# Cross attention block 4: rows of queries and keys interleaved, scores later behind the maxima, another order of loads, half of the last projection inside the block

## The chip, the cores and the metric

One core of one Trainium2 chip runs the whole program. The metric is the device time of one execution in microseconds, of which the span from the first to the last instruction is the larger part. TensorE (PE) multiplies matrices, VectorE (DVE), ScalarE (ACT) and GpSimd (POOL) work elementwise, and DMAs are issued from the queues of SyncE (SP) and of POOL.

## What is computed

Six residual blocks over x of shape (8, 100, 256): self attention with a learned position term, a cross attention, a mixture of experts, a gated scan, a second cross attention, and a projection with ternary weights. The change touches the last two:

```python
def _L1_xattn_ref(query, key, value, mask, ...):   # 16 heads of 16, 8 batches, 100 queries, 361 keys
    q = _split_heads(query @ Wq.T + bq)
    k = _split_heads(key @ Wk.T + bk)
    v = _split_heads(value @ Wv.T + bv)
    scores = jnp.einsum('bhtd,bhsd->bhts', q, k) * scale
    scores = jnp.where(mask[:, None, None, :], scores, -jnp.inf)
    attn = jax.nn.softmax(scores, axis=-1)
    out = jnp.einsum('bhts,bhsd->bhtd', attn, v)
    return out.transpose(0, 2, 1, 3).reshape(...) @ Wo.T + bo

x = x + _L1_xattn_ref(_layernorm(x), ctx_1024, ctx_1024, mask_BxS2_bk0, ...)
x = x + _L1_ffn_ref(_layernorm(x), L1_ffn_weight)   # one 256 x 256 projection
```

## The kernel before

The program counts its blocks from 0: the second cross attention is block 4, the last projection block 5. X holds the residual stream, 100 tokens on partitions for each of 8 batches; a "half" is four batches.

Block 4 works in bf16 with each fp32 number of the queries and keys split into three bf16 parts. Six products of parts (PARTS) are kept, so the contraction of a score has 6 x 16 rows, one row with the mask (ROW_MASK, row 96) and, in the second pass, three rows with the negated row maximum (ROW_MAX, rows 97 to 99). The operands lie in QS (all queries, in region RC) and KS (four slots of one batch each, in regions RBG and RA). The parts go from on-chip memory to DRAM (q_parts, k_parts) and come back, one DMA for each of the six groups of 16 rows: load_queries (L412) and load_keys (L426, and L429 for the mask row). SP issues the queries and keys 0 to 3, POOL keys 4 to 7, each when the scores of the batch two before are over and behind its own four small operations on the maxima.

For each batch and pair of heads, "maxima" (L1259) multiplies queries and keys once and DVE reduces the result to a negated row maximum NM (L1604). POOL splits NM in three (L723 to L726), PE transposes it ("parts", L1270), ACT copies it to NT (L906) and SP stores it in rows 97 to 99 of QS (load_maxima, L419). Then "scores" (L1286) multiplies again, transposed and with the maximum taken off, twelve units in a batch, ACT takes the exponential (L899), "weighted" (L1299) multiplies by the values, and sums_tr (L1311), normalise (L1613, L1614), out_tr (L1319), ot_evac (L920), out_mm (project, L951) and add (L1387) finish the batch. DVE then takes the statistics for the next layer norm (L1350, L1354), POOL the power -0.5 (L598).

The order on each engine comes from a table of ticks, PLAN, walked by run_block4: batch b's entry stands at its tick plus 16 b, and every engine picks its own entries in that order. A tick is no time, only a place in the order. The part of the table before:

```python
        PLAN = ([("maxima", 2 * i, i) for i in range(PAIRS)]
                + [("parts", 21, 0)]
                + [("scores", 28 + TICKS * u // UNITS4, u) for u in range(UNITS4)]
                + [("weighted", max(35 + u // 2, 32 + TICKS * u // UNITS4), u) for u in range(UNITS4)]
                + [("os_evac", 46, 0), ("sums_tr", 49, 0), ("normalise", 49, 0), ("out_tr", 56, 0),
                   ("out_mm", 58, 0), ("add", 59, 0)])
```

After the table block 5 runs: for each half eight transposes (L940), one evacuation to XT (L744), four projections (L951) and four adds, and out goes batch by batch (L570).

## Time and profile before

| | |
|---|---|
| time before, median of 3 (lowest, highest) | 506.22 us (499.56, 510.32) |
| profiled execution: time, span | 508.15 us, 506.4 us |
| mean granted TensorE clock | 0.885 |
| busy over the span | PE 429.4 us (85%), DVE 265.5 (52%), ACT 163.3 (32%), POOL 130.1 (26%) |
| chain that ended last | PE 65%, DVE 11%, DMA 10%, POOL 6%, ACT 4% |
| blocks 0 to 3 | up to 330 us |
| block 4, first maxima to last output projection | 352 to 492 us |

The profile page cuts the span into 40 slices of 12.7 us. The row of TensorE's granted clock reads nine or ten tenths for most slices up to 342 us, and then 5 7 9 5 7 9 5 9 8 9. The chain of waits is read from the last instruction back: at each step to what released it. [...]

### The profile page before, as it was taken

Reading aid. Unit: us, or ns where it says so; the run is one execution under the profiler, and the core shown is the slowest. Engines: PE = TensorE matmul, PEld = TensorE weight load, DVE = VectorE, ACT = ScalarE, POOL = GpSimd, SP = SyncE. Lnnn points to the kernel's source line nnn. Section 1 sums busy time; section 2 is a strip of 40 time slices with the busy share of each in tenths; the row PEclk is TensorE's granted clock in tenths of the full one; section 3 lists DMA queues with packets and bytes.
Section 4 is the critical chain, followed back from the end, with each engine's and each line's share of the span. In section 5 each row is a group of like instructions: output and inputs, shape, how many; then the busy total and the mean of one; then the engine's idle time right before and its main releaser. Section 6 shows DMA issues by size and latency. Waiting matters only on the chain.

```text
span 506.4 us, 7332 instructions
## 1 busy us (share of the span) xinstructions
PE 429.4 (85%) x2920; PEld 280.8 (55%) x2920; DVE 265.5 (52%) x481; ACT 163.3 (32%) x334; POOL 130.1 (26%) x174
## 2 busy tenths in 40 slices
PE   2999986959999974997999999961979969979986
PEld 1556743535667754874555557640346646646654
DVE  5056676992146520236675998651953634643423
ACT  0440430004531231322537424021143534523731
POOL 4620075327441066056100000006003213300100
PEclk9999998969999886999999999995575795975989
DMA  8991020001116963320000029976175256320002
GB/s 242 363 246 37 1 63 27 0 0 45 44 45 192 370 262 113 84 71 20 1 2 0 0 37 134 126 128 90 37 111 75 38 71 91 62 31 2 3 1 65
DMA packets 30616, 42.17 MB, mean 83 GB/s; under 512 B 4330, under 2 KB 27286, under 8 KB 30186
## 3 DMA queue, kind: packets, MB, share of 16 engines
q1 hardware_dynamic: 28279, 35.95, 28.6%
q0 software_dynamic: 2304, 5.76, 7.1%
q8 instruction: 23, 0.38, 0.4%
q14 instruction: 10, 0.08, 0.1%
HBM read 33.00 MB, written 8.98 MB: 83 GB/s over the span
## 4 chain that ended last, share of the span: by engine, by line
PE 65%; DVE 11%; DMA 10%; POOL 6%; ACT 4%; issue 3%; SPq 1%; ACTq 0%; DVEq 0%; POOLq 0%
PE banks L1193 13%; PE banks L1259 6%; PE banks L951 5%; PE banks L1299 5%; PE banks L1286 5%; DMA RC<-NT 4%; PE banks L1006 4%; PE banks L980 3%; PE banks L1227 3%; PE banks L940 2%; DVE RA L449 2%; PE banks L1031 2%; PE banks L1112 2%; PE banks L1130 2%; DMA RC<-q_parts 2%
## 5 line engine op out<-in xcount | busy, mean ns | idle before, releaser
L1604 DVE TENSOR_REDUCE NM<-banks 100x2 f32<-100x722 f32 x64 | 57.2, 906 | 63.2 <-PE banks L1259 62.4
L1193 PE MATMUL banks<-XT,RBG 128*128 128x400 f32 x192 | 65.0, 500 | 2.1 <-ACT XT L744 2.1
L1193 PEld LDWEIGHTS banks<-XT,RBG 128*128 128x128 f32 x192 | 36.3, 190 | 29.8 <-issue 1.2
L899 ACT ACTIVATE CT<-banks 128x400 f32<-128x400 f32 (+1 forms) x72 | 35.9, 504 | 41.9 <-PE banks L1286 40.8
L598 POOL TENSOR_TENSOR rstd<-ve,mhalf 100x4 f32<-100x4 f32 x12 | 12.5, 1040 | 140.0 <-DVE ve L1359 140.0
L744 ACT ACTIVATE XT<-banks 128x800 f32<-128x800 f32 x14 | 11.6, 838 | 98.6 <-PE banks L940 98.6
L1259 PE MATMUL banks<-RBG,RC 97*100 97x361 bf16 x64 | 23.1, 464 | 13.6 <-DMA RC<-q_parts 12.2
L940 PE MATMUL banks<-identf,XN 100*128 100x100 f32 x112 | 17.1, 309 | 17.5 <-DVE XN L1364 10.0
L1299 PE MATMUL banks<-CT,RV 128*17 128x100 f32 (+1 forms) x576 | 28.4, 293 | 0.0
L1286 PE MATMUL banks<-RC,RBG 100*128 100x100 bf16 (+1 forms) x192 | 21.7, 254 | 7.6 <-DMA RC<-NT 7.6
L1286 PEld LDWEIGHTS banks<-RC,RBG 100*128 100x128 bf16 (+1 forms) x192 | 18.3, 140 | 15.4 <-DMA RC<-NT 8.7
L940 PEld LDWEIGHTS banks<-identf,XN 100*128 100x128 f32 x112 | 14.4, 175 | 21.5 <-issue 10.9
L723 POOL CAST NP<-NM 100x16 bf16<-100x16 f32 x8 | 1.6, 196 | 96.2 <-DVE NM L1604 96.2
L980 PE MATMUL banks<-CT,W 128*128 128x361 f32 x64 | 24.5, 536 | 1.9 <-ACT SELT L766 1.9
L1079 PE MATMUL banks<-RC,SELT 128*128 128x400 f32 x64 | 23.7, 518 | 2.7 <-DVE RC L1445 2.4
L1405 DVE TENSOR_TENSOR RC<-RV 128x800 f32<-128x800 f32 x16 | 15.3, 999 | 18.3 <-ACT RV L786 15.9
L1387 DVE TENSOR_TENSOR X<-X,banks 100x256 f32<-100x256 f32 x32 | 13.3, 415 | 21.9 <-PE banks L951 16.9
L1350 DVE BATCH_NORM_STATS2 st<-X 100x6 f32<-100x256 f32 x48 | 19.9, 425 | 7.2 <-DMA X<-in_x 5.8
L636 POOL TENSOR_TENSOR RA<-RA 128x722 f32<-128x722 f32 x6 | 9.0, 1506 | 52.3 <-ACT RA L766 52.3
L991 PE MATMUL banks<-W,CT 128*128 128x256 f32 (+1 forms) x96 | 21.8, 387 | 0.5 <-DVE RC L1533 0.5
L1286 PE MATMUL banks<-RC,RA 100*128 100x100 bf16 (+1 forms) x192 | 18.6, 227 | 4.1 <-DMA RC<-NT 4.1
L1259 PE MATMUL banks<-RA,RC 97*100 97x361 bf16 x64 | 21.5, 429 | 0.0
(228 smaller groups left out, 832.8 us busy)
## 6 DMA issues: line engine op xcount, KB each, us to landing
RA<-in_L_ffn_W SPq DMA_DIRECT2D x2, 2048.0 KB, 11.8
k_parts<-RA SPq DMA_DIRECT2D x18, 180.5 KB, 3.4
RBG<-in_L_attn_W_aiv SPq DMA_DIRECT2D x1, 3072.0 KB, 16.1
CT<-in_ctx_t SPq DMA_DIRECT2D x2, 1444.0 KB, 11.4
RC<-q_parts SPq DMA_DIRECT2D x12, 200.0 KB, 6.7
RBG<-k_parts SPq DMA_DIRECT2D x12, 180.5 KB, 8.8
RA<-k_parts SPq DMA_DIRECT2D x12, 180.5 KB, 9.1
RBG<-k_parts POOLq DMA_DIRECT2D x12, 180.5 KB, 6.5
```

The source lines that it names most:

```text
L899: sc.activation(P4[slot][0:n, g * HG * T:(g + 1) * HG * T], PS[4 + w % 2][0:n, 0:HG * T], ACT.Exp).then_inc(st_exp, 1)
L940: ins = nc.tensor.transpose(PS[2 * g + k][:, j * T:j * T + T], XN[:, b, k * P:(k + 1) * P], identf[0:T, 0:T])
L951: ins = mm(bank[0:T, 0:D], lhs(k), rhs(k), start=(k == 0), stop=(k == KT - 1))
L980: ins = mm((lo, hi)[m][:, 0:S], W4[:, 0, k, m * P:(m + 1) * P], CT[:, k, b * S:(b + 1) * S], start=(k == 0), stop=(k == KT - 1))
L991: ins = mm(o, CT[:, k, b * S + s0:b * S + s0 + n], W4[:, 1, k, :], start=(k == 0), stop=(k == KT - 1))
L1006: ins = mm(PS[4 + i % 2][:, 0:GC], W0[:, w, k, m * P:(m + 1) * P], XT[:, k, GC * g:GC * g + GC], start=(k == 0), stop=(k == KT - 1))
L1079: ins = mm(PS[2 * (u % 3) + g][:, 0:GC], SELT[:, u], AL[:, GB * g:GB * g + GB].rearrange("p s t -> p (s t)"), start=True, stop=True)
L1193: ins = mm(PS[2 * aiv_pair(i) + g][:, 0:GC], WA[:, k, c:c + P], XT[:, k, GC * g:GC * g + GC], start=(k == 0), stop=(k == KT - 1))
L1259: ins = mm(PP[w % 2][0:T, c, 0:S], queries(ROW_MAX, h, b), KS[b % KSLOTS][0:ROW_MAX, h, :], start=True, stop=True)
L1286: ins = mm(PS[4 + w % 2][0:n, c * T:c * T + T], KS[b % KSLOTS][0:KROWS, h, s0:s0 + n], queries(KROWS, h, b), start=True, stop=True)
L1299: ins = mm(PS[6][32 * c:32 * c + VW, g * T:g * T + T], V4[0:n, NJ * b + j, h, :], P4[(NJ * b + j) % PSLOTS][0:n, h * T:h * T + T], start=( ...
L1604: v.tensor_reduce(NM[:, b % 2, 2 * i:2 * i + 2], PP[w % 2][0:T, :, 0:S], AX.X, ALU.max, negate=True).then_inc(mx_out, 1)
```

## The change

Five edits. The rows of part product r go to partitions r, r + 6, r + 12, ... instead of 16 r to 16 r + 15, in QS and KS alike, so the contraction is the same sum in another order. In the table, everything from scores on stands eight ticks later. Keys 2 and 3 are issued after the first half's queries, and keys 3 after the first negated maxima. The half 0 part of block 5 is put into the table at ticks 134 to 146, with semaphores of its own, and the statistics of a batch are closed at once. Waits follow: parts waits for an add three batches back.

```diff
-        PLAN = ([("maxima", 2 * i, i) for i in range(PAIRS)]
-                + [("parts", 21, 0)]
-                + [("scores", 28 + TICKS * u // UNITS4, u) for u in range(UNITS4)]
+                + [("scores", 36 + TICKS * u // UNITS4, u) for u in range(UNITS4)]
...
+        ONCE = ([("ffn_tr", 134, 0), ("ffn_xt", 136, 0)] + [("ffn_mm", 138 + 2 * b, b) for b in range(GB)]
+                + [("ffn_add", 140 + 2 * b, b) for b in range(GB)])
...
-                    queue.dma_start(QS[DK * r:DK * r + DK, g].rearrange("d (k h) n -> d k (h n)", h=HK),
+                    queue.dma_start(QS[r:ROW_MASK:len(PARTS), g].rearrange("d (k h) n -> d k (h n)", h=HK),
...
-                queue.dma_start(KS[s][DK * r:DK * r + DK].rearrange("d (k h) s -> d k (h s)", h=HK),
+                queue.dma_start(KS[s][r:ROW_MASK:len(PARTS)].rearrange("d (k h) s -> d k (h s)", h=HK),
...
-            sp.wait_ge(state, RT)
-            for b in (2, 3):
-                key_ones(b)
-                load_keys(sp, b)
-
             sp.wait_ge(y_mm, 3 * B)
...
+            sp.wait_ge(state, RT)
+            key_ones(2)
+            load_keys(sp, 2)
+            for i in range(3):
+                sp.wait_ge(q4_split1, max(i, 1))
+                store_queries(1, i)
+            for i in range(3):
+                load_queries(sp, 1, i)
             for b in range(B):
 
                 sp.wait_ge(np_out, b + 1)
                 for i in range(3):
                     load_maxima(sp, b, i)
                 if b == 0:
-
-                    for i in range(3):
-                        sp.wait_ge(q4_split1, max(i, 1))
-                        store_queries(1, i)
-                    for i in range(3):
-                        load_queries(sp, 1, i)
+                    key_ones(3)
+                    load_keys(sp, 3)
...
-                if b >= 2:
-                    pe.wait_ge(on_ready, b - 1)
+                if b >= 3:
+                    pe.wait_ge(x_new, 4 * B + b - 2)
...
+            def ffn_tr(_):
+
+                pe.wait_ge(mx_out, PAIRS * B)
+                pe.wait_ge(wf_ready, 1)
+                transposes(5 * B, 0)
+
+            def final(b, bank):
+                pe.wait_ge(xt_ready, 5 * KT * G + KT * (b // GB + 1))
+                for k in range(KT):
+                    ins = mm(bank[0:T, 0:D], XT[:, k, b * T:b * T + T], WN[:, k, :], start=(k == 0),
+                             stop=(k == KT - 1))
+                ins.then_inc(y5_mm, 1)
+
+            def ffn_mm(b):
+                if b >= 2:
+                    pe.wait_ge(x5_new, b - 1)
+                final(b, PS[2 + b % 2])
...
+            pe.wait_ge(x5_new, GB)
+            transposes(5 * B, 1)
+            for b in range(GB, B):
+                final(b, PS[b])
...
-                if L + 1 >= NBLOCKS:
+                if L + 2 == NBLOCKS:
+                    stats(L + 1, b)
+                    aggregate(L + 1, b)
+                    if b == GB - 1:
+                        variance(L + 1, 0)
+                    if b == GB:
+                        norm(L + 1, 0)
+                    if b == B - 1:
+                        variance(L + 1, 1)
+                        norm(L + 1, 1)
                     return
```

How the instructions move, in three places. A row names the line, the operation, its output and inputs by region, the output's shape and how many stand in a row; an fp32 matmul counts once here and twice in the trace. Line numbers of the changed kernel are its own.

TensorE from the last query projection to the first scores, before:

```order
L1239 MATMUL banks<-XT,W 128x400 x4
L1259 MATMUL banks<-RBG,RC 100x361 x22
L1270 MATMUL banks<-identb,NP 48x100
L1259 MATMUL banks<-RBG,RC 100x361 x8
L1286 MATMUL banks<-RC,RBG 128x100 x8
```

and of the change:

```order
L1247 MATMUL banks<-XT,W 128x400 x4
L1267 MATMUL banks<-RBG,RC 100x361 x22
L1278 MATMUL banks<-identb,NP 48x100
L1267 MATMUL banks<-RBG,RC 100x361 x10
L1267 MATMUL banks<-RA,RC 100x361 x6
L1294 MATMUL banks<-RC,RBG 128x100 x4
```

Maxima (L1259, now L1267) come in twos, one pair of heads: 15 pairs stood ahead of the first scores (L1286, now L1294), and now 19; 4 pairs lay between the transpose of the first negated maxima (L1270, now L1278) and the first scores, and now 8.

SP's queue from the loads of keys to the second half's queries, before (keys 2 and 3 go to RA, queries to RC):

```order
L529 DMA RA<-ones_d 3x5776
L426 DMA RA<-k_parts 16x2x2888 x6
L429 DMA RA<-mask_d 1x16x361
L546 DMA RC<-ones_d 1x12800
L525 DMA q_parts<-WX 128x2x400 x3
L412 DMA RC<-q_parts 16x2x3200 x6
L419 DMA RC<-NT 1x16x100 x3
```

and of the change:

```order
L549 DMA RC<-ones_d 1x12800
L533 DMA q_parts<-WX 128x2x400 x3
L420 DMA RC<-q_parts 16x2x3200 x6
L537 DMA RA<-ones_d 3x5776
L434 DMA RA<-k_parts 16x2x2888 x6
L437 DMA RA<-mask_d 1x16x361
L533 DMA q_parts<-WX 128x2x400 x3
L420 DMA RC<-q_parts 16x2x3200 x6
L427 DMA RC<-NT 1x16x100 x3
```

The key loads that stood ahead of the first query store stand behind the first query loads, and the second half's stores and loads moved ahead of the first negated maxima (RC<-NT).

TensorE's end, before (L940 transposes, L951 with WN the last projection):

```order
L1319 MATMUL banks<-identf,zrow 128x100 x2
L951 MATMUL banks<-W,PEM 100x256 x2
L940 MATMUL banks<-identf,XN 128x100 x8
L951 MATMUL banks<-WN,XT 100x256 x8
L940 MATMUL banks<-identf,XN 128x100 x8
L951 MATMUL banks<-WN,XT 100x256 x8
```

and of the change:

```order
L1319 MATMUL banks<-PICK,WQK 100x68 x4
L1327 MATMUL banks<-identf,zrow 128x100 x2
L959 MATMUL banks<-W,PEM 100x256 x2
L948 MATMUL banks<-identf,XN 128x100 x8
L1343 MATMUL banks<-WN,XT 100x256 x8
```

One of the two sets of eight transposes and four projections is gone from the end; it stands between the scores of batches 6 and 7.

## Rows read from the trace of the kernel before

**Rows 1.** The page's costliest groups: line, engine, shapes, count | busy, mean ns | idle before

```profile
L1604 DVE TENSOR_REDUCE NM<-banks 100x2 f32<-100x722 f32 x64 | 57.2, 906 | 63.2 <-PE banks L1259 62.4
```

**Rows 2.** The chain that ended last, in order of time: start us, us, what

```profile
336.31 4.15 DMA q_parts<-WX
...
342.71 9.34 DMA RC<-q_parts
...
373.55 6.71 DMA RC<-NT
...
400.43 0.44 PE banks L1259 x2
...
406.83 8.10 DMA RC<-NT
...
430.33 1.96 PE banks L951 x4
...
441.13 7.79 DMA RC<-NT
```

**Rows 3.** Who waited for whom, 330 to 507 us: total us, times, longest us

```profile
PE banks L1259 <- DMA RC<-q_parts: 12.2, 1, 12.2
PE banks L1286 <- DMA RC<-NT: 11.7, 3, 4.1
```

**Rows 4.** Stretches: length, each engine's busy us (instructions), PEclk, DMA share, GB/s

```profile
12.00:25.00 13.00, 12.16 (x31) 6.69 (x31) 0.46 (x2) 5.50 (x8) 8.83 (x13) 1.00 1.06 366
344.00:350.00 6.00, 0.00 (x0) 0.00 (x0) 0.00 (x0) 0.00 (x0) 5.86 (x4) 0.50 0.98 123
352.10:365.80 13.70, 12.14 (x32) 3.97 (x33) 11.98 (x14) 1.53 (x2) 1.51 (x5) 0.50 0.01 3
381.00:398.00 17.00, 17.00 (x157) 11.12 (x150) 6.14 (x8) 6.73 (x15) 4.45 (x11) 0.50 0.50 68
415.00:432.30 17.30, 17.30 (x160) 11.37 (x161) 6.14 (x8) 6.87 (x15) 4.30 (x11) 0.51 0.46 67
432.30:445.00 12.70, 12.63 (x191) 8.74 (x189) 9.16 (x14) 7.69 (x17) 4.31 (x11) 0.99 0.56 82
449.00:466.10 17.10, 17.10 (x160) 11.28 (x161) 6.14 (x8) 6.87 (x15) 0.82 (x4) 0.52 0.01 2
492.36:506.40 14.04, 9.38 (x48) 6.96 (x46) 5.89 (x17) 1.67 (x2) 1.01 (x1) 0.95 0.20 58
```

**Rows 5.** Short stretches at edges of the granted clock, same columns

```profile
340.00:343.50 3.50, 0.02 (x1) 0.00 (x0) 0.00 (x0) 1.68 (x4) 0.00 (x0) 1.00 0.83 173
343.50:344.50 1.00, 0.00 (x0) 0.00 (x0) 0.00 (x0) 0.37 (x1) 0.56 (x1) 0.60 1.15 134
370.00:372.00 2.00, 2.00 (x40) 1.20 (x33) 1.10 (x2) 0.82 (x2) 0.00 (x0) 0.75 1.07 128
490.50:491.00 0.50, 0.50 (x2) 0.36 (x3) 0.00 (x0) 0.00 (x0) 0.00 (x0) 0.50 0.00 0
```

**Rows 6.** POOL in order of time: start us, us, what

```profile
385.04 3.14 POOL L426 DMA_DIRECT2D RBG<-k_parts  x6
388.13 0.53 POOL L429 DMA_DIRECT2D RBG<-mask_d  x1
```

**Rows 7.** DMA issues (384 to 400 us, then 320 to 507 us): KB each, median us to landing

```profile
RBG<-mask_d POOLq DMA_DIRECT2D x1, 11.3 KB, 8.4
...
q_parts<-WX SPq DMA_DIRECT2D x6, 200.0 KB, 2.5
```

**Rows 8.** The end in order of time: start us, us, engine, what, idle before

```profile
492.36 0.42 DVE L1387 TENSOR_TENSOR X<-X,banks 100x256 f32<-100x256 f32 x1 [3.10 <-PE banks L951]
...
494.79 1.38 DVE L1364 TENSOR_SCALAR XN<-X,mv,rstd 100x256 f32<-100x256 f32 x4 [1.13 <-POOL rstd L598]
...
498.17 0.85 PE L940 MATMUL banks<-identf,XN 100*128 100x100 f32 x8
...
500.01 3.70 PE L951 MATMUL banks<-WN,XT 128*100 128x256 f32 x16 [0.99 <-ACT XT L744]
```

More of the change, by code:

```diff
@@ L246, in build @@
         qs_one = sem("qs_one")
-        ks_one = sem("ks_one")
+        ks_one = [sem(f"ks_one{i}") for i in range(KSLOTS)]
+        y5_mm = sem("y5_mm")
+        x5_new = sem("x5_new")
         ks_ld = [sem(f"ks_ld{b}") for b in range(B)]
@@ L390, in build @@
                 + [("parts", 21, 0)]
-                + [("scores", 28 + TICKS * u // UNITS4, u) for u in range(UNITS4)]
-                + [("weighted", max(35 + u // 2, 32 + TICKS * u // UNITS4), u) for u in range(UNITS4)]
-                + [("os_evac", 46, 0), ("sums_tr", 49, 0), ("normalise", 49, 0), ("out_tr", 56, 0),
-                   ("out_mm", 58, 0), ("add", 59, 0)])
-        PLAN_END = TICKS * (B - 1) + 60
-        ORDER = ("parts", "sums_tr", "normalise", "out_tr", "out_mm", "maxima", "scores", "weighted",
-                 "os_evac", "add")
+                + [("scores", 36 + TICKS * u // UNITS4, u) for u in range(UNITS4)]
+                + [("weighted", max(43 + u // 2, 40 + TICKS * u // UNITS4), u) for u in range(UNITS4)]
+                + [("os_evac", 54, 0), ("sums_tr", 57, 0), ("normalise", 57, 0), ("out_tr", 64, 0),
+                   ("out_mm", 66, 0), ("add", 67, 0)])
+        PLAN_END = TICKS * (B - 1) + 68
+        ONCE = ([("ffn_tr", 134, 0), ("ffn_xt", 136, 0)] + [("ffn_mm", 138 + 2 * b, b) for b in range(GB)]
+                + [("ffn_add", 140 + 2 * b, b) for b in range(GB)])
+        ORDER = ("parts", "sums_tr", "normalise", "out_tr", "out_mm", "ffn_tr", "ffn_mm", "maxima", "scores",
+                 "weighted", "os_evac", "ffn_xt", "add", "ffn_add")
         def run_block4(**own):
@@ L405, in run_block4 @@
                             own[name](b, x)
+                    for n, at, x in ONCE:
+                        if n == name and name in own and tick == at:
+                            own[name](x)
         def load_queries(queue, g, i):
@@ L921, in ot_evac @@
                 ins.then_inc(ot_out, 1)
-            run_block4(scores=exps, parts=parts_out, os_evac=os_evac, out_tr=ot_evac)
-            xt_out(xn_tr, 5 * G, xt_ready)
+            run_block4(scores=exps, parts=parts_out, os_evac=os_evac, out_tr=ot_evac,
+                       ffn_xt=lambda _: xt_out(xn_tr, 5 * G, xt_ready, [0]))
+            xt_out(xn_tr, 5 * G, xt_ready, [1])
         @block.tensor
@@ L1245, in _ @@
             pe.wait_ge(qs_one, 16)
-            pe.wait_ge(ks_one, 16 * KSLOTS)
             pe.wait_ge(xt_ready, 5 * KT * G)
@@ L1251, in maxima @@
                 if i == 0:
+                    pe.wait_ge(ks_one[b % KSLOTS], 16)
                     pe.wait_ge(ks_ld[b], 16 * (len(PARTS) + 1))
@@ L1306, in sums_tr @@
                 pe.wait_ge(os_out, b + 1)
-                pe.wait_ge(np_out, min(B, b + 2))
+                pe.wait_ge(np_out, min(B, b + 3))
                 if b >= 1:
@@ L1324, in out_mm @@
                 project(4 * B + b, lambda k: OT[b % 2][:, k], lambda k: W4[:, 3, k, :], Y4)
-            run_block4(maxima=maxima, parts=parts_tr, scores=scores, weighted=weighted,
-                       sums_tr=sums_tr, out_tr=out_tr, out_mm=out_mm)
-            pe.wait_ge(wf_ready, 1)
-            for b in range(B):
-                if b % GB == 0:
-                    transposes(5 * B, b // GB)
-                    pe.wait_ge(xt_ready, 5 * KT * G + KT * (b // GB + 1))
-                if b >= 3:
-                    pe.wait_ge(x_new, 5 * B + b - 3)
-                project(5 * B + b, lambda k: XT[:, k, b * T:b * T + T], lambda k: WN[:, k, :], PS[4 + b % 4])
+            def ffn_tr(_):
[12 more added lines that the diff above has]
+                final(b, PS[2 + b % 2])
+            run_block4(maxima=maxima, parts=parts_tr, scores=scores, weighted=weighted,
+                       sums_tr=sums_tr, out_tr=out_tr, out_mm=out_mm, ffn_tr=ffn_tr, ffn_mm=ffn_mm)
+            pe.wait_ge(x5_new, GB)
+            transposes(5 * B, 1)
+            for b in range(GB, B):
+                final(b, PS[b])
         @block.vector
@@ L1615, in normalise, with final_add @@
                                 ).then_inc(on_ready, 1)
-            run_block4(maxima=row_max, normalise=normalise, add=lambda b, _: add(4, b, Y4))
-            for b in range(B):
-                add(5, b, PS[4 + b % 4])
+            def final_add(b, bank):
+                dve.wait_ge(y5_mm, b + 1)
+                v.tensor_tensor(X[:, b], X[:, b], bank[0:T, 0:D], ALU.add).then_inc(x5_new, 1)
+            run_block4(maxima=row_max, normalise=normalise, add=lambda b, _: add(4, b, Y4),
+                       ffn_add=lambda b: final_add(b, PS[2 + b % 2]))
+            for b in range(GB, B):
+                final_add(b, PS[b])
 _OUT = (B, T, D)
```

4 lines of the change are left out of this document (2 added, 2 removed).

## Prediction

> **What bounds the kernel now.** I read the two coarse parts of the page first (busy shares, and the span in slices) and then the chain that ended last. TensorE carries most of that chain, and nothing that the change touches runs before 317 us, so the question is the last 170 us: block 4 (the second cross attention) and the final projection. There the chain names two kinds of wait. Before the first row maxima of block 4 TensorE stands 12.2 us until queries are loaded [rows 3], of which 4.15 us is the store of a query part and 9.34 us the six loads [rows 2]. Three more times, at 373.6, 406.8 and 441.1 us, the chain runs through the small load of the negated maxima into the query tile (6.7 to 8.1 us on the way) [rows 2]. TensorE stands only 11.7 us for it in all three together [rows 3], because the first part of each transfer lies under scores still queued.
>
> The third view is the table of stretches [rows 4], and it shows what those three stops really cost. [...] Each low stretch begins just after one of the three stops, and each does 157 to 160 records in 17.0 to 17.3 us. So block 4 runs two batches in 34 us: one stop of 4 us, one batch at the low clock, one at the high clock. VectorE's row maxima take 0.906 us a pair of heads [rows 1], 7.2 us for a batch, so VectorE is not the bound at either clock; it is the bound only where TensorE has nothing but maxima (352 to 366 us, 11.98 of 13.7 us busy) [rows 4].
>
> **The change, part by part.** The profiled execution took 508.15 us, about 2 us above the median of 506.22; the sum is made against 508.15.
>
> *The eight ticks.* The transpose of batch b's negated maxima stands at tick 21 of that batch. The scores that need them stood at tick 28 and now stand at 36: 15 ticks of cover where there were 7. A batch is 16 ticks. At the high clock 191 records are about 1.1 batches, so a batch is 11.4 us and a tick 0.71 us; 15 ticks are 10.7 us against at most 8.1 us of transfer. At 7 ticks it was 5.0 us, which is why it stalled. I therefore take all three stops away, **-11.7 us** [rows 3]. With them goes what started the low stretches. At the high rate (12.7 us for 191 records, 66.5 ns each) the 157, 160 and 160 records take 10.4, 10.6 and 10.6 us in place of 17.0, 17.3 and 17.1 [rows 4]: **-19.7 us**. The bound on the other side is zero, if the clock falls at something else.
>
> The price of the eight ticks: 19 pairs of maxima run alone in place of 15. The stretch of 15 lasted 13.7 us [rows 4], so four more at VectorE's 0.92 us a pair is +3.7 us; those four no longer stand in the mix, where a pair is 0.44 us at the high clock [rows 2]: -1.8 us. Net **+1.9 us**. At the end the last scores run without maxima beside them, but that is TensorE work all the same and is counted.
>
> *The rows in spread order.* Each load writes 16 partitions. They were neighbours, and are now six apart over 96. While only such loads run, the core moves 123 GB/s with its DMA engines busy 0.98 of the time; a stretch of 128-partition loads moves 366 GB/s at the same busy share [rows 4]. So the engines wait on something that the narrow target causes. The effect of spreading has no row. Below, it is nothing (9.34 us stays); above, it is the wide rate (about 3.2 us). I take twice the rate, 4.7 us, since 16 of 96 rows is still a small target: -4.6 us. [...]
>
> *The load order.* Keys 2 and 3 left the queue ahead of the queries. The first query store took 4.15 us against a median of 2.5 us for such stores [rows 2, 7]; I take 1.1 us of it. First maxima at about 346.5 us: together **-5.7 us** (bounds -1 and -7.5). What is late next: keys 2 follow the query loads and are due after 16 pairs, 14.7 us, enough. The first negated maxima now queue behind the second half's query loads and are due 17.3 us after the start; up to 1 us may be lost there, not counted. POOL's loads of keys 4 to 7 wait for the scores of the batch two before. Those are over at tick 50 and the keys are due at tick 64: 14 ticks, 10.0 us at the high clock. Before, such a set took from 385.04 to 388.13 + 8.4 = 396.5 us, 11.5 us [rows 6, 7]. This is the tight spot: with doubled transfers it is about 7.5 us and hidden; unspread, it would be late by 1.5 us.
>
> *The final projection of half 0 inside.* Its transposes and four projections cost 0.85 + 3.70 us at the high clock [rows 8], now in the queue of a TensorE that has no room: +4.55 us. What leaves the end: from the last add of block 4 to the span's end was 14.0 us [rows 4]. The chain that remains is add to end of normalising, 492.36 to 496.17 [rows 8], then 0.3 of transposes, 0.95 of evacuation, 3.8 of projections, 2.65 to the end: 11.5 us, so -2.5 us. But TensorE, which used to fill the 4 us of VectorE and POOL work with half 0, now stands in it. After TensorE stopped at 340 us (0.02 us busy in the next 3.5) its granted clock was down at 343.5 to 344.5 us (0.60) [rows 5], and a projection at the low clock takes 1.96 us [rows 2] against 0.93. All four and the transposes low would be +4.7 us, none 0. After the lowering at 490.5 us [rows 5] the tail was back at 0.95 on average [rows 4], so I take +2.6 us. This part together: **+4.65 us**. [...]
>
> Sum: 508.15 - 11.7 - 19.7 + 1.9 - 5.7 + 4.65 = **477.6 us**.
>
> **Rivals.**
> *The clock comes back late or falls once more.* Each low stretch ended right at an output projection (430.33 us, 1.96 us of wide fp32 matmuls, then high at 432.3) [rows 2, 4]; the first, between 370 and 372 us, did not [rows 5]. If the start of the new mix stays low until the first output projection, tick 66, then 30 ticks (21 us at 0.71) take 1.6 times as long: +12 us, **490 us**. For it: nothing in the maxima alone keeps TensorE full. Against: it rose by 372 us under the same mix, some 5 us after the first scores.
> *Spreading changes nothing.* Start 4.6 us later, keys 4 to 7 late by 1.5 us each: +10.6 us, **488 us**. For: no row shows a spread load. Against: the two plateaus.
> *Slower than before.* The same late keys, but each of the four waits lets the clock fall for a batch, 6.6 us on top of 1.5 us: 477.6 + 4.6 + 4 x 8.1 = **515 us**. It decides if a key set takes over 10 us. Against: a wait of 1.5 us is shorter than the three that lowered the clock (3.8 to 4.1), and at a low clock the ticks are longer, so the wait heals itself.
> *The gain is smaller all round* (VectorE's adds delay the maxima, short waits for ScalarE: half of the 31.4 us that stops and clock give would be lost, **493 us**). Against: VectorE is busy 9.16 of 12.70 us in a stretch at the high clock [rows 4], it has room.
>
> **Numbers.** Forecast 0.64 (own range 468 to 485), late clock 0.16, spreading without effect 0.09, smaller gain 0.07, slower 0.04. The range 467 to 492 holds the first three but for their tails. What a measurement here can tell from no change is about 2%, 10 us: faster 0.92, within 0.06, slower 0.02.
>
> **What would show it.** The first maxima at 345 to 348 us and query loads landing in about 5 us; more than 180 GB/s while only keys or queries load; no wait of scores for the load of negated maxima; granted clock near 1.0 from some 5 us after the first scores to the end of block 4; a batch every 11 to 12 us; TensorE idle 4 us before the last transposes with the clock low after. The forecast is wrong if the clock stays at 0.5 with TensorE busy, or if maxima of batches 4 to 7 wait for keys.

## The result, and the profile after

The changed kernel takes **479.84 us** (median of four runs, 478.36 to 483.51). The kernel before, run beside it, took 506.63 us (median of four, 499.56 to 510.32): a ratio of 0.953, 95% interval 0.941 to 0.965. 477.6 us was forecast, with a range of 467 to 492. Medians here are of all runs of a kernel; ratios and their intervals leave out the slower ones (in spread 476.85 and 478.45 us, at granted clocks of 0.928 and 0.932, against 469.57 to 472.21 us at 0.938 to 0.942). The profiled execution took 480.73 us, its span 479.0 us, at a mean granted clock of 0.922 against 0.885.

From the page after: the busy shares, the granted clock in 40 slices of 12 us, and the row that answers to [rows 1]. The clock's row of the page before, in slices of 12.7 us, stands first.

```profile
PEclk9999998969999886999999999995575795975989
```

```profile
PE 411.9 (86%) x2920; PEld 270.2 (56%) x2920; DVE 266.2 (56%) x481; ACT 162.6 (34%) x334; POOL 131.1 (27%) x174
...
PEclk9999998897999979589999999999955999999976
...
L1635 DVE TENSOR_REDUCE NM<-banks 100x2 f32<-100x722 f32 x64 | 57.1, 906 | 25.0 <-PE banks L1267 24.0
```

The same 2920 matmul records now keep TensorE busy 17.5 us less. From 342 us on the row before reads 5 5 7 5 7 9 5 9 7 5 9 8 9, 13 digits (above, where the profile before is told, three of them are missing). That alternation is gone: two low slices where queries load and maxima stand alone, nines after that, a low end. VectorE's reduce is unchanged at 906 ns, but stood 24.0 us for scores where it stood 62.4.

The chain in order of time (start us, us, what):

```profile
344.85 4.42 DMA RC<-q_parts
349.41 0.82 PE banks L1267 x2
...
387.25 1.04 PE banks L959 x4
...
398.82 1.04 PE banks L959 x4
...
415.56 0.92 PE banks L1319 x8
...
427.14 0.92 PE banks L1319 x8
...
467.05 1.58 PE banks L948 x8
...
469.60 6.67 PE banks L1343 x16
```

The query loads take 4.42 us in place of 9.34 [rows 2]. The first maxima start at 349.41 us; this execution ran 2.2 us later than the one of before upstream of the change, so that is 347.2 on the scale of before. From one batch to the next it is 11.58 us (387.25 to 398.82, 415.56 to 427.14). No piece is a load of negated maxima. The last transposes and projections (L948, L1343) stand at the end with half a set less, and slow.

Who waited for whom between 330 and 480 us (total us, times, longest us):

```profile
PE banks L1267 <- DMA RC<-q_parts: 7.2, 1, 7.2
...
PE banks L948 <- DVE XN L1386: 3.0, 1, 3.0
```

12.2 us became 7.2, and the 11.7 us for RC<-NT [rows 3] has no row any more. Stretches of after, in the columns of [rows 4]:

```profile
346.00:350.00 4.00, 0.59 (x2) 0.45 (x3) 0.00 (x0) 0.00 (x0) 3.85 (x4) 0.50 0.96 241
366.90:373.30 6.40, 6.40 (x66) 4.53 (x67) 4.31 (x6) 3.32 (x8) 0.00 (x0) 0.51 0.23 53
373.30:450.00 76.70, 75.85 (x1159) 52.80 (x1152) 49.31 (x81) 47.05 (x105) 20.02 (x53) 1.00 0.26 67
461.90:475.70 13.80, 9.69 (x27) 6.49 (x28) 3.84 (x11) 0.87 (x2) 1.01 (x1) 0.51 0.05 15
464.06:479.00 14.94, 8.23 (x24) 5.63 (x24) 4.26 (x12) 0.84 (x1) 1.01 (x1) 0.61 0.10 27
```

241 GB/s moves where 123 moved, at the same busy share. The first scores start at 366.74 us. The clock is up about 6.5 us later and stays up for 77 us, with TensorE busy 75.85 of 76.70 us. From 461.9 to 475.7 us it is down, and that holds nearly the whole end. It fell at the last output projection of block 4, before TensorE's wait for the last normalising (3.0 us): in the 2 us ahead of it TensorE had 0.52 us of work, and no single wait there was longer than 0.81 us.

```profile
460.00:462.00 2.00, 0.52 (x5) 0.22 (x3) 0.68 (x2) 0.58 (x2) 0.00 (x0) 0.99 0.00 0
462.00:464.00 2.00, 2.00 (x4) 0.98 (x4) 0.00 (x0) 0.00 (x0) 0.00 (x0) 0.50 0.00 0
```

### The profile page after: what moved, and what is told of

It is laid out like the page before. It is cut to its first block, busy times and chain, and to the rows that moved or that the text cites. A ratio compares the mean times of both kernels' runs of the same rounds, so it can differ in the third digit from the quotient of the medians.

```text
span 479.0 us, 7340 instructions
## 1 busy us (share of the span) xinstructions
PE 411.9 (86%) x2920; PEld 270.2 (56%) x2920; DVE 266.2 (56%) x481; ACT 162.6 (34%) x334; POOL 131.1 (27%) x174
## 3 DMA queue, kind: packets, MB, share of 16 engines
q1 hardware_dynamic: 28279, 35.95, 24.8%
## 4 chain that ended last, share of the span: by engine, by line
PE 64%; DVE 12%; issue 9%; POOL 5%; DMA 4%; ACT 4%; SPq 1%; POOLq 0%; DVEq 0%; ACTq 0%
PE banks L1201 14%; PE banks L1267 5%; PE banks L1014 4%; PE banks L999 4%; PE banks L1307 3%; PE banks L988 3%; PE banks L1294 3%; PE banks L959 3%; PE banks L1235 3%; DVE RA L457 2%; PE banks L948 2%; PE banks L1039 2%; PE banks L1120 2%; PE banks L1138 2%; PE banks L1181 2%
## 5 line engine op out<-in xcount | busy, mean ns | idle before, releaser
L605 POOL TENSOR_TENSOR rstd<-ve,mhalf 100x4 f32<-100x4 f32 x12 | 12.7, 1056 | 150.6 <-DVE ve L1381 150.6
L751 ACT ACTIVATE XT<-banks 128x800 f32<-128x800 f32 x14 | 11.6, 839 | 99.0 <-PE banks L948 99.0
L948 PE MATMUL banks<-identf,XN 100*128 100x100 f32 x112 | 17.3, 310 | 22.9 <-DVE XN L1386 13.6
L948 PEld LDWEIGHTS banks<-identf,XN 100*128 100x128 f32 x112 | 14.3, 175 | 27.6 <-issue 15.1
L1267 PE MATMUL banks<-RBG,RC 97*100 97x361 bf16 x64 | 21.0, 426 | 8.8 <-DMA RC<-q_parts 7.2
L1087 PE MATMUL banks<-RC,SELT 128*128 128x400 f32 x64 | 24.7, 538 | 2.7 <-DVE RC L1476 2.4
L988 PE MATMUL banks<-CT,W 128*128 128x361 f32 x64 | 23.4, 516 | 1.9 <-ACT SELT L773 1.9
L1436 DVE TENSOR_TENSOR RC<-RV 128x800 f32<-128x800 f32 x16 | 15.3, 1005 | 17.3 <-ACT RV L793 15.0
L1307 PE MATMUL banks<-CT,RV 128*17 128x100 f32 (+1 forms) x576 | 24.5, 258 | 0.0
L1564 DVE TENSOR_TENSOR RC<-banks,RC 100x256 f32<-100x256 f32 x8 | 3.4, 424 | 33.0 <-PE banks L1190 33.0
L1386 DVE TENSOR_SCALAR XN<-X,mv,rstd 100x256 f32<-100x256 f32 x48 | 18.2, 441 | 6.1 <-POOL rstd L605 6.0
L1087 PEld LDWEIGHTS banks<-RC,SELT 128*128 128x128 f32 x64 | 13.1, 207 | 12.8 <-DVE RC L1476 3.0
L959 PE MATMUL banks<-W,RA 128*100 128x256 f32 x32 | 10.3, 453 | 11.2 <-DVE X L1418 6.7
L999 PEld LDWEIGHTS banks<-W,CT 128*128 128x128 f32 (+1 forms) x96 | 17.5, 184 | 4.0 <-DVE RC L1564 0.9
L1490 DVE TENSOR_TENSOR RC<-banks,RV 128x800 f32<-128x800 f32 x16 | 15.5, 977 | 7.6 <-PE banks L1087 7.6
## 6 DMA issues: line engine op xcount, KB each, us to landing
RA<-in_L_ffn_W SPq DMA_DIRECT2D x2, 2048.0 KB, 12.2
CT<-in_ctx_t SPq DMA_DIRECT2D x2, 1444.0 KB, 11.4
```

Source lines behind the costliest of these rows:

```text
L948: ins = nc.tensor.transpose(PS[2 * g + k][:, j * T:j * T + T], XN[:, b, k * P:(k + 1) * P], identf[0:T, 0:T])
L959: ins = mm(bank[0:T, 0:D], lhs(k), rhs(k), start=(k == 0), stop=(k == KT - 1))
L988: ins = mm((lo, hi)[m][:, 0:S], W4[:, 0, k, m * P:(m + 1) * P], CT[:, k, b * S:(b + 1) * S], start=(k == 0), stop=(k == KT - 1))
L999: ins = mm(o, CT[:, k, b * S + s0:b * S + s0 + n], W4[:, 1, k, :], start=(k == 0), stop=(k == KT - 1))
L1087: ins = mm(PS[2 * (u % 3) + g][:, 0:GC], SELT[:, u], AL[:, GB * g:GB * g + GB].rearrange("p s t -> p (s t)"), start=True, stop=True)
L1267: ins = mm(PP[w % 2][0:T, c, 0:S], queries(ROW_MAX, h, b), KS[b % KSLOTS][0:ROW_MAX, h, :], start=True, stop=True)
```

## The experiments

The kernel before was timed again beside each group of kernels; its median was 502.07 us beside ticks8, spread, nospread and nofinal, 505.59 beside order, spread_order, stall4 and stall3, 508.06 beside filler, ticks4 and nofinal_warm, and 505.81 beside busy_maxima. It was 506.63 us beside the changed kernel. So medians of different groups can differ by 6.0 us (502.07 and 508.06) with nothing changed, and ratios are the safer measure between groups.

What happens before block 4 differs between executions too: its first maxima start between 346.42 (filler) and 358.59 us (nospread). So it helps to read distances inside one trace, in us, each from a single execution:

| kernel | first maxima to first output projection | on to the last one | on to the end |
|---|---|---|---|
| before | 43.6 | 94.6 | 16.0 |
| changed | 37.8 | 74.8 | 17.0 |
| ticks8 | 41.5 | 87.3 | 17.4 |
| spread | 33.3 | 73.0 | 17.3 |
| nospread | 45.8 | 91.6 | 16.6 |
| order | 41.3 | 91.6 | 14.5 |
| spread_order | 33.6 | 72.7 | 14.6 |
| nofinal | 36.8 | 70.1 | 16.1 |
| filler | 44.5 | 74.8 | 14.6 |
| stall4 | 38.0 | 83.1 | 16.5 |
| stall3 | 38.3 | 80.2 | 16.3 |
| ticks4 | 44.0 | 73.2 | 18.5 |
| nofinal_warm | 37.0 | 70.0 | 17.4 |
| busy_maxima | 33.1 | 70.0 | 17.4 |

### The eight ticks alone (ticks8)

```diff
-                + [("scores", 28 + TICKS * u // UNITS4, u) for u in range(UNITS4)]
+                + [("scores", 36 + TICKS * u // UNITS4, u) for u in range(UNITS4)]
```

The rest of the table behind the scores moves by eight as well, and two waits move by a batch, as in the change.

> The kernel before with the eight ticks alone (rows in blocks of 16, old load order, block 5 at the end). My theory: the three stops of scores for the negated maxima (11.7 us) go, and the low stretches behind them (19.7 us) with them, 1.9 us is paid for the longer stretch of maxima alone, and keys 4 to 7 come 1.5 us late each because unspread loads take 11.5 us and 14 ticks are 10.0 us: 506.6 - 11.7 - 19.7 + 1.9 + 6 = about 483 us, granted clock 1.0 over most of block 4. Rival: each late key lowers the clock as the old stops did; then nearly all of the gain is lost, 500 to 515 us, with low stretches in four batches.

Measured: 503.22 us (median of 10), ratio 0.999 (0.993 to 1.004): no gain that the runs can show. (In the table its profiled execution is 9.4 us shorter in block 4 than the one of before; that of before, at 508.15 us, was one of the long ones of its kernel.) The chain, and the waits that the scores' place in the order was to end:

```profile
388.20 8.41 DMA RBG<-mask_d
404.65 7.71 DMA RBG<-mask_d
...
421.26 8.40 DMA RA<-mask_d
438.65 7.33 DMA RA<-mask_d
```

```profile
PE banks L1259 <- DMA RBG<-mask_d: 5.8, 2, 3.3
...
PE banks L1259 <- DMA RA<-mask_d: 5.2, 2, 3.0
```

Three stops for negated maxima became four for keys, 11.0 us in all, 3.3 at most (RBG and RA hold the key slots, and the mask row is the last load of a set). In its stretches TensorE has 0.68 us of work between 393 and 397 us, and what follows the stops runs partly low (0.86 in the second row here, 0.78 from 411 to 430 us, 0.80 from 430 to 460 us):

```profile
393.00:397.00 4.00, 0.68 (x6) 0.44 (x6) 0.46 (x1) 0.83 (x3) 0.83 (x4) 1.00 0.27 34
397.00:409.00 12.00, 11.93 (x163) 8.12 (x161) 7.61 (x11) 6.12 (x13) 3.50 (x7) 0.86 0.54 82
```

A key set still takes 11.5 us (385.1 to 388.2 + 8.4). TensorE ran out of work at 393.3 us, so the cover was 8.2 us. I had given it 10.0.

### The spread rows alone (spread)

```diff
-                    queue.dma_start(QS[DK * r:DK * r + DK, g].rearrange("d (k h) n -> d k (h n)", h=HK),
+                    queue.dma_start(QS[r:ROW_MASK:len(PARTS), g].rearrange("d (k h) n -> d k (h n)", h=HK),
...
-                queue.dma_start(KS[s][DK * r:DK * r + DK].rearrange("d (k h) s -> d k (h s)", h=HK),
+                queue.dma_start(KS[s][r:ROW_MASK:len(PARTS)].rearrange("d (k h) s -> d k (h s)", h=HK),
```

> The kernel before with the spread rows alone. My theory: query loads land in about 4.5 us instead of 9.3 (start 4.6 us earlier), key loads are off the queues in 5 us instead of 9, so the negated maxima land within about 3 to 5 us of their issue against 5.0 us of cover at seven ticks; the three stops shrink to 0 to 1.5 us and the low stretches mostly vanish: 506.6 - 4.6 - 9 - 15 = about 478 us, almost all of the whole change. Rival: seven ticks are still too few, a stop of 1 to 3 us stays in odd batches and lowers the clock each time as before: 506.6 - 4.6 - 5 = about 497 us, and the eight ticks carry the rest.

Measured: 472.21 us (median of 5, 469.57 to 478.45), ratio 0.936 (0.928 to 0.943). Two lines do at least as much as the whole change. Its scores stand seven ticks behind the transpose of negated maxima, as before. The loads that follow on it, in its chain, and its waits for them:

```profile
396.31 4.28 DMA RC<-NT
408.26 4.79 DMA RC<-NT
420.75 4.19 DMA RC<-NT
```

```profile
PEld banks L1286 <- DMA RC<-NT: 3.0, 5, 1.1
PE banks L1286 <- DMA RC<-NT: 1.3, 3, 0.8
```

The 3 KB load lands in 4.2 to 4.8 us where it took 6.7 to 8.1 [rows 2]. Nothing was done to this load itself. The loads of keys and queries, which run beside it (in the kernel before the DMA engines were busy 0.66 of the 8.10 us in which it was under way), land in 3.9 us in the median where they took 5.9 to 6.7; that it is late because of them is read from this, not measured by itself. Seven ticks, 5.0 us, cover it. What is left is 0.8 us at most of matmul waiting (1.1 of weight loading), and the clock does not fall there:

```profile
372.00:400.00 28.00, 27.86 (x438) 19.28 (x435) 19.65 (x26) 17.48 (x39) 8.78 (x22) 1.00 0.41 102
400.00:450.00 50.00, 47.71 (x755) 32.83 (x758) 32.07 (x57) 31.13 (x71) 11.29 (x31) 1.00 0.20 48
```

### All but the spread rows (nospread)

The changed kernel with the two lines of spread put back.

> The changed kernel with the rows put back in blocks of 16, all else kept. My theory (the rival of the prediction that I gave 9 in 100): start 4.6 us later, maxima of batches 4 to 7 wait 1.5 us each for keys: 479.8 + 10.6 = about 490 us, clock kept at 1.0. Rival 1: the waits for keys lower the clock too, 479.8 + 4.6 + 4 x 8.1 = about 517 us. Rival 2: rows do not matter to the transfers, 480 us.

Measured: 513.96 us (median of 4), ratio 1.022 (1.014 to 1.031): slower than before. The slow rival's 515 us is what the other four edits give without the first. Its chain:

```profile
352.96 14.53 DMA q_parts<-WX
...
371.41 8.97 DMA RC<-NT
...
399.12 3.27 issue
...
426.94 0.92 PE banks L1319 x8
...
443.89 0.92 PE banks L1319 x8
```

```profile
PE banks L1267 <- issue: 12.0, 4, 3.3
```

The second half's store waits 14.53 us among loads, the first negated maxima land after another 8.97, and four waits ahead of maxima (their releaser unnamed; they stand at the first maxima of batches 4 to 7, where keys are waited for) take 12.0 us. The batch shown takes 16.95 us, 5.4 more than with spread rows: 3.0 of waiting, the rest a lower clock (0.80 over this batch, where it was 1.00 in the changed kernel). My rival had put 1.5 and 6.6 for these. From the first maxima to the last output projection it is 24.8 us more than in the changed kernel: 12.0 of waits for keys, one wait of 4.3 us for the first negated maxima, and 8.5 of lower clock (0.82 over that distance against 0.89, with TensorE busy 115.85 us where it was 107.33). The rival had 32.4 us for keys and clock and nothing for the negated maxima.

### The load order alone (order), and with the spread rows (spread_order)

In short:

```diff
-            for b in (2, 3):
-                key_ones(b)
-                load_keys(sp, b)
...
+            key_ones(2)
+            load_keys(sp, 2)
+            for i in range(3):
+                sp.wait_ge(q4_split1, max(i, 1))
+                store_queries(1, i)
+            for i in range(3):
+                load_queries(sp, 1, i)
```

> The kernel before with the new order of loads alone (rows in blocks, scores at tick 28, block 5 at the end). My theory: the first query store comes about 1 us earlier, but with unspread loads the first negated maxima now queue behind keys 2 and the second half's queries and the first scores wait some 4 to 8 us for them; the stop of batch 1 goes in exchange (3.8 us and its low stretch of 6.6). About 500 us, within 1% of before. Rival: the order by itself is worth its 1 us and the stop of batch 1: 490 us.

> The kernel before with the spread rows and the new order of loads, scores at tick 28, block 5 at the end: the changed kernel without its two costly parts. My theory: 471 us, as the spread rows alone (472.2) or 1 us better, and about 3 us below the run without block 5 inside (475.1), which differs from it by the eight ticks alone: those cost their 1.9 us and save nothing once the loads are quick. Rival: the eight ticks still hide waits of 1 us or so for the negated maxima in each batch, and this one comes out at 476 us or above.

Measured: order 506.58 us (median of 10), ratio 0.998 (0.993 to 1.004). spread_order 475.76 us (median of four that lie far apart, 468.35 to 487.42; no interval is given), so no gain over the spread rows alone is shown. In order the first load of negated maxima comes late, as in nospread:

```profile
PE banks L1285 <- DMA RC<-NT: 18.6, 5, 8.4
```

18.6 us where it was 11.7 [rows 3]. The queries gained nothing by the order: TensorE waited 12.2 us for them as before, and with spread rows 7.0 us (spread_order) against 7.2 (spread).

### Half 0 of block 5 at the end again (nofinal)

```diff
-        ONCE = ([("ffn_tr", 134, 0), ("ffn_xt", 136, 0)] + [("ffn_mm", 138 + 2 * b, b) for b in range(GB)]
-                + [("ffn_add", 140 + 2 * b, b) for b in range(GB)])
+        ONCE = []
```

and both halves run behind the table, as before.

> The changed kernel with both halves of block 5 at the end again, all else kept. My theory: half 0 inside costs TensorE 4.55 us that it has not got to spare, and the end did not get shorter, since with TensorE idle ahead of the last transposes the last projections run at the low clock (15.0 us from the last add of block 4 to the end, against 14.0 before): 479.8 - 4.55 - 1.0 = about 474 us. Rival: the scores of the last batches leave gaps in which half 0 is free, and its removal from the end is worth 2.5 us: about 482 us.

Measured: 475.12 us (median of 4), ratio 0.947 (0.941 to 0.954). Against 479.84 us the part costs 4.7 us by the medians; 4.65 was the forecast. The medians are of different groups, and the ratios differ by 0.005 (some 3 us), within both intervals, so the traces have to tell. From the output projection of batch 4 to that of batch 5 the changed kernel takes 14.02 us (433.17 to 447.19) and nofinal 9.26 (431.71 to 440.97), with the clock at 1.00 in both: **4.76 us** for half 0, which stands there. The other distances between output projections agree within 0.11 us. The end is no shorter for it, 17.0 us against 16.1, in a column of the table that runs from 14.5 to 18.5 us where both halves stand at the end. (nofinal keeps the statistics closed at once; that edit was never tried alone.)

### TensorE kept busy before the last transposes (filler)

The changed kernel with nine fp32 matmuls whose result nobody reads:

```diff
             pe.wait_ge(x5_new, GB)
+            for i in range(9):
+                mm(PS[0][:, 0:D], WN[:, 0, 0:P], WN[:, 1, :], start=True, stop=True)
             transposes(5 * B, 1)
```

> The changed kernel with nine fp32 matmuls into an unused bank ahead of the last transposes (their result is not used), so that TensorE stands idle for less while VectorE and POOL normalise half 1. My theory: the end costs 15.0 us from the last add because TensorE's idle time keeps the clock at 0.5 through the last projections (6.66 us where 3.70 at the high clock); with the filler the clock is back before them: 479.8 - 3 = about 476.5 us. Rival: the clock stays low all the same (it fell before, in the gaps of the last batch) and nothing changes: 480 us, or 1 us worse where the filler delays the transposes.

Measured: 481.31 us (median of 4, 478.42 to 485.0), ratio 0.955 (0.933 to 0.977). In the stretch from the last add of block 4 to the end:

```profile
467.75:480.30 12.55, 8.88 (x42) 6.87 (x41) 4.26 (x12) 0.84 (x1) 1.02 (x1) 0.95 0.11 33
...
384.00:388.00 4.00, 4.00 (x58) 2.73 (x60) 2.50 (x4) 1.51 (x3) 0.00 (x0) 0.63 0.02 4
```

The end took 12.55 us against 14.94: its low clock was worth 2.4 us (2.6 was in the sum). Here too the clock fell ahead of the last output projection, at about 465.5 us (0.99 in the 2.5 us before, 0.50 in the 2.25 us after); the filler did not keep it up, it brought it back. The median did not get better. The second row is the place: this execution stayed low (0.50, with TensorE busy all the time) until about 387 us, some 23 us behind its first scores (363.72 us) where the changed kernel's profile had 6.5. That is the late clock of my first rival, in a kernel that does nothing new before 467 us, so it is chance from run to run. Its price is in the first column of the table: 44.5 us against 37.8, 6.7 us.

### A wait put in on purpose (stall4, stall3)

POOL gets four, or three, operations of 1.7 us ahead of the last part of batch 6's negated maxima; their result is not read again.

```diff
+                if b == 6:
+                    for _ in range(4):
+                        link(gp.tensor_tensor(QW, QW, QP[:, 0], ALU.subtract))
                 gp.tensor_tensor(NP[:, i, 2], NM[:, i], NP[:, i, 1], ALU.subtract).then_inc(np_ready, 1)
```

> The changed kernel with four operations of 1.7 us put into POOL's chain ahead of batch 6's third part of the negated maxima (on a scratch buffer, nothing left out), so that TensorE waits 3 to 4 us there and the load for it still lands in time. My theory of the low stretches (a stop of that length lowers the clock, and it stays low with TensorE busy until the next output projection): wait 3.6 us and 13 ticks low, 5 us more: about 488 us. Rival: the low stretches had another cause (power, or the mix of work) and a wait costs its own length only: 483.5 us, clock 1.0 behind it.

> The same with three operations: TensorE waits about 1.9 us at batch 6. My theory: too short to lower the clock, 479.8 + 1.9 = about 482 us with the clock at 1.0 behind it. Rival: any stop near 2 us lowers it too: 487 us. In the kernel with the eight ticks alone waits of 3.0 to 3.3 us lowered it, so the edge lies below 3 us if this one does, and between 1.9 and 3 if not.

Measured: stall4 488.89 us, stall3 487.50 us (four runs each), ratios 0.966 (0.960 to 0.972) and 0.966 (0.961 to 0.970); by the medians 9.0 and 7.7 us more than the changed kernel, whose own interval, from another group, reaches to 0.965. The wait and the clock in stall4:

```profile
PE banks L1281 <- POOL NP L736: 3.9, 1, 3.9
```

```profile
430.00:432.00 2.00, 0.66 (x6) 0.42 (x6) 0.05 (x1) 0.25 (x1) 1.21 (x2) 0.61 0.00 0
...
440.00:442.00 2.00, 2.00 (x42) 1.23 (x31) 0.68 (x2) 0.92 (x3) 0.00 (x0) 0.83 0.04 8
```

and in stall3:

```profile
PE banks L1281 <- POOL NP L736: 2.5, 1, 2.5
```

```profile
430.00:438.00 8.00, 8.00 (x94) 5.70 (x88) 4.32 (x6) 3.38 (x7) 0.00 (x0) 0.57 0.02 3
438.00:444.00 6.00, 6.00 (x95) 4.09 (x92) 3.14 (x8) 4.08 (x10) 1.82 (x5) 1.00 0.00 0
```

After one wait of 3.9 us TensorE works for some 9 us at the low clock (0.50 from 431.3 to 440.4 us). The distance between the two output projections around it is 18.92 us where the changed kernel has 11.27: 7.65 us for wait and clock together. In stall3 it is 16.50 us: 5.2 us, of which 2.5 are the wait. The rest of the 9.0 and 7.7 us lies within the spread of runs. I had expected stall3 to wait about 1.9 us and keep the clock. It waited 2.5 us, and lost it, for about 7 us. So a wait of 2.5 us was enough here and waits of 0.8 us (spread) were not; what lies between wasn't tried. But the length of one wait does not tell all: at the end of block 4 the clock fell behind three waits of 0.6 to 0.8 us with little work between them. Both low stretches ended ahead of an output projection: my reading that a low stretch lasts until one is wrong.

### Four ticks for eight (ticks4)

nofinal with scores at 32, and what follows them four ticks earlier too.

> The changed kernel without block 5 inside and with four ticks in place of eight (scores at 32). My theory: two pairs of maxima fewer run alone, -0.9 us, and 11 ticks (7.8 us) still cover the load of the negated maxima (2.9 to 4.8 us), so no stop: 475.1 - 0.9 = about 474 us with a spread between runs as small as without block 5 inside (2.8 us). Rival: 11 ticks already let single runs fall into a stop, as at 7 ticks (468 to 487 us): the runs lie 8 us or more apart.

Measured: 479.49 us (median of 4, 474.24 to 486.21), ratio 0.948 (0.927 to 0.969), an interval that holds all of nofinal's. Its profile is the slowest of the four, and shows the late clock once more:

```profile
376.00:380.00 4.00, 4.00 (x44) 2.24 (x40) 1.82 (x2) 1.47 (x3) 1.61 (x6) 0.50 0.01 2
...
388.00:390.00 2.00, 2.00 (x34) 1.22 (x32) 0.91 (x1) 0.61 (x2) 0.00 (x0) 0.60 0.00 0
```

Low until about 389 us, with TensorE busy nearly all the while (it waited 0.6 us in one place). The run is 12.0 us over the fastest of the same kernel, but the late clock is not all of that: up to the first output projection it costs 44.0 us against 36.8 in nofinal, about 7 us. The runs favour neither eight ticks over four nor four over none. In the traces a batch takes 12.0 us with four ticks, 11.6 to 12.5 with none (spread) and 11.57 with eight; eight cost 3.5 us more than none up to the first output projection and give 2.9 back up to the last.

### TensorE kept busy before and between the maxima (nofinal_warm, busy_maxima)

nofinal with 14 fp32 matmuls, result unread, while the queries load; and busy_maxima with one more ahead of each of the pairs 1 to 17:

```diff
+            for i in range(14):
+                mm(PS[0][:, 0:D], W4[:, 3, 0, 0:P], W4[:, 3, 1, :], start=True, stop=True)
...
+                if 1 <= w <= 17:
+                    mm(PS[4][:, 0:D], W4[:, 3, 0, 0:P], W4[:, 3, 1, :], start=True, stop=True)
```

> The changed kernel without block 5 inside, with 14 fp32 matmuls into a bank that is free while TensorE waits for the first queries (their result is not used). My theory: the clock is then high as the maxima begin, but TensorE is busy for less than half of the maxima alone, so it falls there and the start of the mix stays as it was: 475 us, no change. Rival: it holds through the 17 us of maxima, and the 4 to 5 us of the mix that run at the low clock now run at the high one: 473 us, with row maxima still 0.92 us a pair.

> The kernel of the last run (no block 5 inside, 14 matmuls under the wait for queries) with one further fp32 matmul of 256 columns ahead of each of the next 17 pairs of maxima, into a bank that the scores use later (nothing reads it). What is open: single runs of every variant differ by up to 12 us in how late after the first scores the clock rises (372 us in one profile, 387 to 389 in two others). My theory: with TensorE busy for 0.85 of 0.92 us a pair the clock, high from the matmuls under the wait, holds through the maxima, and the mix starts high in every run: about 471 us, all runs within 4 us. Rival: it falls in the maxima all the same; then a pair and the extra matmul take 1.3 to 1.7 us at the low clock instead of VectorE's 0.92 and the run is 7 to 14 us slower, 480 us or more.

Measured: nofinal_warm 473.0 us (median of 5), ratio 0.938 (0.922 to 0.953); busy_maxima 474.49 us (median of 6, 470.87 to 476.44), ratio 0.946 (0.940 to 0.952). In nofinal_warm the clock was high until the maxima began and fell in them, with TensorE busy 0.86 us in the 2 us before the row and 1.34 in its own:

```profile
350.00:352.00 2.00, 1.34 (x4) 0.49 (x4) 1.88 (x3) 0.00 (x0) 2.00 (x2) 0.66 1.04 234
```

In busy_maxima it never fell, in the maxima or at the start of the mix:

```profile
352.00:356.00 4.00, 4.00 (x22) 2.50 (x21) 4.00 (x6) 0.00 (x0) 1.40 (x2) 1.00 0.72 194
...
364.00:368.00 4.00, 4.00 (x66) 2.62 (x65) 3.81 (x6) 3.18 (x8) 0.00 (x0) 1.00 0.58 133
```

So with work between the maxima the clock stayed up, and in this execution the first output projection came 33.1 us after the first maxima, 3.7 us earlier than in nofinal. It is the fastest of its six runs, and a gain in their times is not shown: all medians from 472 to 475 us lie within each other's spread. That the late start can no longer happen isn't proved either: its six runs lie within 5.6 us, but so do the four of nofinal, within 2.8.

## Why the prediction held, point by point

*The total* held for a partly wrong reason. 480.73 against 477.6 us is 3.1 us: 2.2 that this execution was late upstream, 0.7 in the start and 0.8 in the end make 3.7, and the rest of block 4 came out 0.6 us shorter than summed.

*The step that failed: "The eight ticks ... I therefore take all three stops away, -11.7 us", and with them -19.7 us of low clock.* The two amounts were right as amounts: no wait for RC<-NT is left, and from the first maxima to the last output projection it is 112.6 us where it was 138.2, 25.6 less, against 24.95 in the sum (11.7 + 19.7 less 1.9 and 4.55). But they belong to the spread rows. I had costed those at -4.6 us, by the query loads alone. What I missed is that the same two lines shorten every load beside which the small load of negated maxima runs, and that this load then lands sooner too (3.4 us in the median in spread, 5.1 in the kernel before). The hint was there: 6.7 to 8.1 us [rows 2] for 3 KB. Seven ticks would have covered a transfer of up to 5.0 us, and I never asked whether spreading brings it there. ticks8 (0.999) and spread (0.936) settle it.

*The price of the eight ticks*, +1.9 us, can't be told from zero by the runs of spread_order and nofinal. In their traces the way from the first maxima to the last output projection is 106.3 and 107.0 us: 0.7 us, after about 1 us of waits for negated maxima that the ticks take away. That fits the 1.9.

*The tight spot.* Right in kind and place, wrong in size: about 3 us late per key set unspread (11.0 and 12.0 us for four in ticks8 and nospread), not 1.5, because the cover is 8.2 us, not 10.0. I had counted 14 ticks at the mean of 0.71 us; those between the scores and the keys took 0.59. With spread rows the set takes the 7.5 us forecast, 412.24 to 415.30 + 4.4 us, under that cover; POOL in the profile after, in the columns of [rows 8]:

```profile
412.24 3.08 POOL L434 DMA_DIRECT2D RA<-k_parts  x6 [2.02 <-PE banks L1294]
415.30 0.50 POOL L437 DMA_DIRECT2D RA<-mask_d  x1
```

and its DMA issues from 338 to 480 us (KB each, median us to landing):

```profile
RC<-NT SPq DMA_DIRECT2D x24, 3.1 KB, 2.9
...
RA<-mask_d POOLq DMA_DIRECT2D x2, 11.3 KB, 4.4
```

By the cover of ticks8, 0.7 us of room is all there is. The first of these rows is the load of negated maxima: 2.9 us in the median, against 5.1 in the kernel before.

*Spreading doubles the rate.* Right: 241 GB/s against 123 [rows 4]; 4.42 us for the six query loads where 4.7 was taken. Twice was an estimate, between no effect and the threefold rate (366 GB/s) of the 128-partition loads [rows 4].

*The start*, 347.2 us on the scale of before against 346.5, is right in sum and wrong in one term. The gain is 5.0 us against 5.7, and 4.9 of it are the query loads, so the 1.1 us for the order did not show: spread, with the old order, waits 7.2 us for its queries like the changed kernel. What an earlier store may give, slower issuing takes: SP needs 0.59 us to issue a spread load where it needed 0.42, 1.1 us more for the six. I had also read the 4.15 us of the store as part of TensorE's 12.2 us of waiting, but TensorE stopped at 340.02 us and the store landed at 340.46. First scores 17.3 us after the first maxima against 17.3: right. *A batch* of 11.58 us against 11.4: right.

*Half 0 inside.* Right: 4.76 us in the trace for its 4.55 of TensorE work, and an end that got no shorter, against 4.65 in all. By its terms: the end took 14.94 us where 11.5 + 2.6 = 14.1 was summed, all four last projections at the low clock (6.67 us against 3.70 [rows 8]); the filler gives 2.4 us of that back. The one edit that was forecast to be a loss is one. What I had wrong is why the end runs low: not the 3.0 us in which TensorE stands before the last transposes, since the clock had fallen at 461.9 us, in the last batch of block 4. The kernel before fell there too (490.5 us [rows 5]) and came back over the work of half 0 (0.53 from 492 to 494 us, 1.00 from 494 to 496), which the change took away. This trace shows no more than that the clock, already at 0.50, stayed there through the 3.0 us; it does not show a fall by them.

*Rivals.* The late clock came about in single runs (filler, ticks4), but at 6.7 to 7 us, not at 12: it came back some 23 to 25 us after the first scores, and the 12 were worked out for a low stretch of some 34. "Spreading changes nothing" and "slower" are both nospread, at 513.96 us: the slow rival's 515 is what spreading saved this change from. Its sum was near for a partly wrong reason: less for each key set than I had put, and in its place the wait for the first negated maxima and an execution that came 4.4 us later to block 4. I gave it 0.04 because "a wait of 1.5 us is shorter than the three that lowered the clock"; the waits were twice that, and one of 2.5 us was enough (stall3).

*What stays open.* What ends a low stretch. They lasted 7 to 17 us with TensorE busy nearly all through, in single runs from the first maxima to 389 us, and no run here shows what decides. Which of the kernels between 472 and 475 us is best is open too. Spread rows alone is the plainest of them. It beats the kernel before; against the changed kernel its ratio is lower (0.936 against 0.953), with intervals that just overlap.

## What to carry over

Price a change to one transfer by everything that runs beside it and queues behind it: the 3 KB of negated maxima took up to 8.1 us [rows 2] in the kernel before and 2.9 us in the median in the changed one, with nothing done to their load, and here the cure was in the loads beside it, not in more slack. Try each edit of a bundle alone: here one of five carried the gain, and without it the others made the kernel slower than before. A stop in front of a full TensorE can cost more than its length: 2.5 us of waiting cost 5.2, because the engine worked on at a granted clock of 0.57 for the next 8 us (stall3). Compare distances inside the traces when medians of separate timings differ by less than the same kernel does between them.

## What the runs showed of the chip

- Loads into 16 neighbouring partitions moved 123 GB/s (kernel before), into 16 that lie six apart 241 GB/s (changed kernel), at about the same busy share of the DMA engines (0.98 and 0.96). SP took 0.42 us to issue one of the first and 0.59 us for one of the second.
- After a single wait of 2.5 us TensorE's clock was low for about 7 us (stall3, 0.57 over the 8 us from 430 us), after one of 3.9 us for some 9 us of work (stall4, 0.50), after those of 3.8 to 4.1 us in the kernel before for 17 (0.50 to 0.52); with waits of at most 0.8 us in a full TensorE it stayed at 1.00 (spread). In the last batch of block 4 it fell after three waits of 0.6 to 0.8 us in close order, with 0.52 us of work in the last 2 us (changed kernel).
- In maxima bound by VectorE (busy 11.36 of the 12 us from 354 us) the clock fell from 1.00 to 0.50 (nofinal_warm: 0.86 us of TensorE work in 2 us, 1.1 of them a wait for queries, and then 1.34 in 2), and came back only in the mix, at 371 us; with one small fp32 matmul ahead of each pair it stayed at 1.00 (busy_maxima).
- With the same program and the same work ahead of it, the clock came up about 6.5 us after the first scores in one execution (changed kernel) and some 23 us after them in another (filler). That made 6.7 us of difference.
